# Two node stages of a graph attention kernel: merges by head with the residual in them, and eight PSUM banks in the last stage

## The chip, the cores and the metric

The kernel runs on one core of one Trainium2 chip. The metric is the device time of one execution in microseconds (us). The names of the engines in the rows are PE (TensorE), PEld (its weight loads), DVE (VectorE), ACT (ScalarE), POOL (GpSimd) and SP (SyncE, which issues the DMAs of the node stages); a q behind a name, as in DVEq or SPq, is that engine's sequencer.

## The reference

Three graph attention layers over 6,250 nodes with 256 features and 100,000 edges: two of a GATv2 block with 4 heads of 64 channels, then one of a GAT block with 8 heads of 32. Each block ends in a residual and a layer norm.

```python
def _gatv2_layer(x, src, dst, n, Wl, Wr, att, b):
    ...
    msg = xl[src] * alpha[:, :, None]
    out = jax.ops.segment_sum(msg, dst, num_segments=n)
    return out.reshape(n, H * C) + b
...
x = _layernorm(x + _L0_gnn_ref(x, edge_index, ...), axis=-1)
x = _layernorm(x + _L1_gnn_ref(x, L1_gnn_W, L1_gnn_a, src, dst), axis=-1)
```

In a GATv2 layer each node also has an edge to itself (a loop), and its message is what the kernel calls a node's own row.

## The kernel before

The nodes lie in 49 tiles of 128. The program goes through four node stages (`node_dve(l)`, `node_pe(l)` and so on, l = 0 to 3) with an edge stage between each two of them. An edge stage gathers rows by indirect DMA, scores them, and adds weighted rows into `acc`, 128 partitions by 49 tiles by 264 words. This change touches the node stages with l = 2 (the third stage) and l = 3 (the last).

A node stage is a software pipeline over tiles, written by `tiles(eng, (part, lag), ..., ring=R)`: at step t each engine runs its parts in the order of the list, each for tile t - lag. Buffers are taken in turn, tile t has buffer t % R. The first steps are written out, the middle ones are a hardware loop (`Fori`) whose body is R steps, the last are written out again. Every engine has a queue of its own and executes it strictly in order; engines meet by semaphores alone.

**Third stage (l = 2).** It ends layer two, makes the first layer norm, and the products of layer three. Per tile:
- SP loads the node's own row `own` (L490) and the residual row `res` of x (L492), and stores the projected table row (L504, lag 8) and the normalised row `hx_dram` (L508, lag 6): four DMAs a tile, each about 130 KB.
- DVE, for two tiles at once (`merged_two`): `own` = `own` times the loop's weight `wx` (L1342), `tmp` = `acc` times the weight `wn` (L1343), wait, `tmp` = `tmp` + `own` (L1345). Weights are spread over the 64 channels of a head by a zero step. Then `stats` (lag 2): bn_stats (L1372) and bn_aggr (L1374), one tile each. At the front of an even step stands `finish` (lag 4): a reciprocal of the root (L1384) and -mean/std (L1387), for two tiles.
- ACT: `normal` (lag 4, L758) writes the normalised tile from PSUM, `root` (lag 2, L767) takes the square root for two tiles, L790 and L792 copy products, L774 copies a transposed tile.
- PE: `products` (lag 5, L987), `turn_h` (lag 4, L974), then `residual`: a bias product (L957) and the product of `res` with the identity (L958), then `total`: `tmp` times the identity (L962), all summed in one of four PSUM banks.
- POOL clears `acc` of each merged tile (L630) and a part of x3 (L628), behind `acc_read`, which the merge raises.

**Last stage (l = 3).** SP loads `res` from `hx_dram` (L492) and stores the output (L501, lag 6). DVE runs `finish` (lag 4), `merged_two` (one tensor_tensor for two tiles, L1337) and `stats` (lag 2); ACT `normal` and `root`; PE `residual` (L958) and `total` (L962), in four banks. PE waits for `h_ready` of tile t - 4 before it opens a bank again, and DVE's `finish` waits for `std_ready`, which ACT's `root` raises when both `bn_aggr` of the pair have run.

## Time and profile before

| | before |
|---|---|
| median of 3 runs | 4010.43 us (4007.61 to 4011.79) |
| profiled execution, its own time | 4004.83 us |
| its span | 4003.0 us |
| PE, DVE, ACT, POOL busy | 88%, 82%, 32%, 69% of the span |
| third stage, first merge to last merge | 2647.6 to 2779.8 us |
| last stage, first merge to last merge | 3914.8 to 3993.7 us |

The span is what the profiler saw from the first to the last instruction; 1.8 us of the execution's own time lie outside it. Nearly all of the span is in the three edge stages, which the change does not touch. What it touches are about 147 us (the third stage, from its first merge to its last store) and 88 us (the last). A row of a timeline gives the start, the time taken, the engine, the line, the operation, what it writes and reads, and in brackets how long the engine had been idle and what ended that.

### The profile page before, as it was taken

The page shows a single profiled execution, that of the slowest core. Times are in us where ns is not written, and L with a number is a line of the kernel's source. Part 1 is how long each engine was busy: PE and PEld are TensorE (multiplying, and loading weights), DVE is VectorE, ACT ScalarE, POOL GpSimd, SP SyncE. Part 2 cuts the span into 40 slices and gives each one's busy share as a digit, 9 for nine tenths or more (in the row PEclk, how much of TensorE's full clock was granted, in tenths as well). Part 3 has the DMA queues.
Part 4 walks back from the last instruction along what each step waited for, and adds up shares of the span by engine and source line. Part 5 has one row for each costly group of instructions (what it writes and reads, how often), then busy time and mean ns, then how long its engine had stood idle before and what let it go on. Part 6 is the DMA issues. An engine that isn't in the chain of part 4 may idle for free. (4 is left out here: it accounts for less than half of the span.)

```text
span 4003.0 us, 115501 instructions
## 1 busy us (share of the span) xinstructions
PE 3522.5 (88%) x30761; PEld 2584.0 (65%) x30762; DVE 3296.9 (82%) x10046; ACT 1278.9 (32%) x4356; POOL 2765.2 (69%) x3039
## 2 busy tenths in 40 slices
PE   6699999999999668999999999977678888787885
PEld 5577777777777456777777777745445555555543
DVE  6768888888888885888888888876688898888886
ACT  4433333333333463333333333324111111111113
POOL 5577777777776467777777777723777777777760
PEclk9899999999999899999999999989799999899989
DMA  4344444444443124444444444435455555555544
GB/s 99 116 131 136 136 131 136 136 135 132 134 136 106 58 70 135 136 135 131 136 136 135 131 136 136 131 96 186 134 143 140 143 145 143 141 144 138 144 109 129
DMA packets 279405, 520.84 MB, mean 130 GB/s; under 512 B 98391, under 2 KB 165121, under 8 KB 279313
## 3 DMA queue, kind: packets, MB, share of 16 engines
q0 software_dynamic: 120320, 338.39, 31.2%
q1 hardware_dynamic: 158993, 181.36, 15.1%
q8 instruction: 41, 0.67, 0.1%
q14 instruction: 51, 0.42, 0.0%
HBM read 484.05 MB, written 35.46 MB: 130 GB/s over the span
## 5 line engine op out<-in xcount | busy, mean ns | idle before, releaser
L704 POOL DMA_INDIRECT gathered<-table,idx x2496 | 2501.4, 1002 | 787.6 <-issue 526.0
L1120 PE MATMUL pS<-gathered,Dm 128*128 128x264 f32 x4992 | 1689.5, 422 | 107.7 <-DVE Dm L1533 58.9
L1520 DVE TENSOR_TENSOR acc_mem<-acc_mem,pS 128x264 f32 x2496 | 1043.6, 418 | 144.8 <-PE pS L1120 105.6
L1059 PE MATMUL pZ<-DT,x 128*128 128x128 bf16 x9984 | 1090.2, 221 | 14.1 <-DVE DT L1480 11.5
L1059 PEld LDWEIGHTS pZ<-DT,x 128*128 x9984 | 874.2, 98 | 325.0 <-issue 51.7
L873 ACT ACTIVATE reluT<-pZ 128x256 f32<-128x256 f32 x1664 | 637.1, 383 | 1128.5 <-PE pZ L1065 1098.6
L1120 PEld LDWEIGHTS pS<-gathered,Dm 128*128 128x128 f32 x4992 | 797.2, 200 | 239.5 <-DVE gathered L1551 104.9
L1065 PE MATMUL pZ<-ident,gathered 128*128 128x128 f32 x3328 | 934.6, 281 | 11.9 <-DMA gathered<-table,idx 11.8
L1551 DVE TENSOR_TENSOR gathered<-gathered 128x256 f32<-128x256 f32 x2496 | 941.6, 417 | 1.8 <-ACT gathered L865 1.0
L1533 DVE TENSOR_TENSOR Dm<-pS,rel_items 128x256 f32<-128x256 f32 x1239 | 513.8, 415 | 0.0
L1065 PEld LDWEIGHTS pZ<-ident,gathered 128*128 128x128 f32 x3328 | 470.4, 141 | 16.2 <-DMA gathered<-table,idx 14.3
L1051 PEld LDWEIGHTS pL<-DT,x 128*128 x2496 | 236.0, 105 | 217.5 <-issue 116.5
L1051 PE MATMUL pL<-DT,x 128*128 128x128 bf16 x2496 | 324.7, 236 | 37.5 <-ACT first_row L859 28.5
L1073 PE MATMUL pL<-reluT,attpad 128*32 128x128 f32 x6656 | 269.2, 280 | 0.1
L1565 DVE TENSOR_TENSOR_SCAN F<-flags,cT 128x128 f32<-128x128 f32 x156 | 67.4, 432 | 216.6 <-ACT cT L858 214.8
L987 PE MATMUL pS<-W,gathered 128*128 128x260 f32 (+1 forms) x588 | 174.3, 421 | 36.1 <-ACT gathered L774 34.1
L1073 PEld LDWEIGHTS pL<-reluT,attpad 128*32 128x32 f32 x6656 | 156.9, 109 | 51.1 <-ACT reluT L873 0.9
L617 POOL TENSOR_TENSOR pool_pad<-zeros 128x1 f32<-128x1 f32 x184 | 54.6, 297 | 194.4 <-DVE gathered L1345 120.7
L841 ACT ACTIVATE lin<-gathered 128x128 f32<-128x128 f32 x52 | 21.8, 418 | 444.9 <-DMA gathered<-table,idx 444.9
L987 PEld LDWEIGHTS pS<-W,gathered 128*128 128x128 f32 x588 | 104.9, 198 | 75.9 <-ACT gathered L774 55.0
L1480 DVE TENSOR_SCALAR DT<-DT,iota_part 128x2048 bf16<-128x2048 bf16 x156 | 117.1, 750 | 12.4 <-DMA DT<-rel_dram 12.3
L1088 PE MATMUL pL<-ident,lin 128*128 128x128 f32 x156 | 53.1, 340 | 77.1 <-ACT lin L841 77.0
(230 smaller groups left out, 3211.4 us busy)
## 6 DMA issues: line engine op xcount, KB each, us to landing
DT<-rel_dram SPq DMA_DIRECT2D x156, 512.0 KB
gathered<-table,idx POOLq DMA_INDIRECT x2496
table<-xls SPq DMA_DIRECT2D x147, 132.0 KB, 2.0
flags<-flag_dram SPq DMA_DIRECT2D x416, 32.0 KB
flags<-flag_dram SPq DMA_DIRECT2D x52, 256.0 KB
gathered<-table SPq DMA_DIRECT2D x98, 132.0 KB, 2.1
gathered<-in_x SPq DMA_DIRECT2D x98, 128.0 KB, 2.1
hx_dram<-gathered SPq DMA_DIRECT2D x49, 128.0 KB, 1.7
```

Of the source, the lines that this page charges most:

```text
L704: nc.gpsimd.indirect_dma_start(out=G[:, b, i, :], out_offset=None, in_=tab[l], in_offset=bass.IndirectOffsetOnAxis(ap=idx[:, b, i:i + 1], ...
L873: nc.scalar.activation(relu_slot(i), z_slot(i), ACT.Relu).then_inc(relu_done, 1)
L987: mm = nc.tensor.matmul(pX[:, b, 0:width], hT[:, b, q * P:(q + 1) * P], W[:, q, 0:width], start=(q == 0), stop=(q == 1))
L1051: mm = nc.tensor.matmul(pL[:, 0:P], s3[:, bass.ds(tk[i], 1), s, GI - 1 - i:9 * GI - 1 - i].rearrange("p o c -> p (o c)"), moving, start=(i ...
L1059: mm = nc.tensor.matmul(z_slot(i)[:, half], x3[:, bass.ds(tk[i], 1), s, half].rearrange("p o c -> p (o c)"), moving, start=(s == 0), stop= ...
L1065: mm = nc.tensor.matmul(z_slot(i)[:, half], G[:, b, i, half], ident[:], is_transpose=True, start=False, stop=True)
L1073: nc.tensor.matmul(pL[a * (P // Q):(a + 1) * (P // Q), 0:P], attpad[:, q, ATT0 - k:ATT0 - k + P // Q], relu_slot(Q * k + a)[:, q * P:(q + ...
L1120: nc.tensor.matmul(pS[:, i % 4, 0:ROW], Dm[:, i % 8, :], G[:, at[0], at[1], :], start=True, stop=True).then_inc(seg_done, 1)
L1480: v.tensor_scalar(DT[:, b, :], DT[:, b, :], iota_part[:, 0:1], None, ALU.is_equal).then_inc(dt_ready, 1)
L1520: link(v.tensor_tensor(acc_at(n), acc_at(n), pS[:, n % 4, 0:ROW], ALU.add))
L1533: ins = v.tensor_tensor(Dm[:, 2 * p % 8:2 * p % 8 + 2, :], numbers.unsqueeze(1).to_broadcast([P, 2, P]), rel.unsqueeze(2).to_broadcast([P, ...
L1551: ins = v.tensor_tensor(gv, gv, row[:, D:D + H].unsqueeze(2).to_broadcast([P, H, D // H]), ALU.mult)
```

## The change

In the last stage the sums take eight PSUM banks in place of four, and `residual` loads go into eight buffers (`res8`). The ring is eight, so a bank is opened again behind tile t - 8. DVE's order at an even step becomes `merged_two`, `finish`, `stats`. Stores have lag 11; the normalised tiles still go through four buffers.

In the third stage the merge goes by tile and head: for each tile and each of 4 heads `own` = `own` times `wx` + `res`, one scalar_tensor_tensor over 128x64 whose weight is a pointer scalar in SBUF; behind a wait, `tmp` = `acc` times `wn` + `own` in the same form. `acc_read` is raised behind each tile. The residual product with the identity falls away, the bias product stays. SP's loads wait for `acc_read` of tile t - 4 in place of `sum_ready`.

The buffers are laid out anew in the same space. Cut to what matters:

```diff
-        pSum = [pS[:, 2, 0:D], pS[:, 3, 0:D], pL[:, 0:D], pM[:, 0:D]]
+        pSum = [pS[:, 2, 0:D], pS[:, 3, 0:D], pL[:, 0:D], pM[:, 0:D],
+                pS[:, 0, 0:D], pS[:, 1, 0:D], pZ[:, 0, 0:D], pZ[:, 1, 0:D]]
...
-                        else:
-                            sp.wait_ge(sum_ready, t + ((l - 2) * TILES - 3))
+                        elif l == 2:
+                            sp.wait_ge(acc_read, t + ((l - 1) * TILES - 3))
...
+                    if l == 3:
+                        if not (static(t) and t < 8):
+                            sp.wait_ge(sum_ready, t + (TILES - 7))
+                        sp.dma_start(res8[:, b, :], hx_dram[rows(t), :]).then_inc(res8_in[b], 16)
...
-                    tiles(sp, (load, 0), (store, 6), ring=4)
+                    tiles(sp, (load, 0), (store, 11), ring=8)
...
-                    tiles(act, (normal, 4), (root, 2), ring=4)
+                    tiles(act, (normal, 4), (root, 2), ring=8)
...
                 def residual(t, b, h):
-                    pe.wait_ge(res_in[b], (h + (l - 2) * QUARTER[b] + 1) * 16)
-                    if not (static(t) and t < 4):
-                        pe.wait_ge(h_ready, t + ((l - 1) * TILES - 3))
                     if l == 2:
+                        if not (static(t) and t < 4):
+                            pe.wait_ge(h_ready, t + (TILES - 3))
                         nc.tensor.matmul(pSum[b], ones_bf, bias3, start=True, stop=False)
-                    nc.tensor.matmul(pSum[b], ident[:], res[:, b, :], start=(l == 3), stop=False)
+                    else:
+                        pe.wait_ge(res8_in[b], (h + 1) * 16)
+                        if not (static(t) and t < 8):
+                            pe.wait_ge(h_ready, t + (2 * TILES - 7))
+                        nc.tensor.matmul(pSum[b], ident[:], res8[:, b, :], start=True, stop=False)
...
                         for k in range(n):
                             dve.wait_ge(own_in[b + k], (h + (HALF[b + k] if b + k < 2 else 0) + 1) * 16)
-                        mine = by_head(own[:, of, 0:D])
-                        v.tensor_tensor(mine, mine, spread_heads(wx), ALU.mult)
-                        v.tensor_tensor(by_head(tmp[:, of, :]), by_head(num), spread_heads(wn), ALU.mult).then_inc(node_step, n)
+                            dve.wait_ge(res_in[b + k], (h + 1) * 16)
+                            for j in range(H):
+                                of = slice(j * C, (j + 1) * C)
+                                ins = v.scalar_tensor_tensor(own[:, b + k, of], own[:, b + k, of], wx[:, bass.ds(t + k, 1), j],
+                                                             res[:, b + k, of], ALU.mult, ALU.add)
+                        ins.then_inc(node_step, n)
                         dve.wait_ge(node_step, t + ((l - 1) * TILES + n))
-                        v.tensor_tensor(tmp[:, of, :], tmp[:, of, :], own[:, of, 0:D], ALU.add).then_inc(acc_read, n)
+                        for k in range(n):
+                            num = acc[:, bass.ds(t + k, 1), 0:D].rearrange("p o r -> p (o r)")
+                            for j in range(H):
+                                of = slice(j * C, (j + 1) * C)
+                                ins = v.scalar_tensor_tensor(tmp[:, b + k, of], num[:, of], wn[:, bass.ds(t + k, 1), j],
+                                                             own[:, b + k, of], ALU.mult, ALU.add)
+                            ins.then_inc(acc_read, 1)
...
-                else:
+                elif l == 2:
                     tiles(dve, (finish, 4), (merged_two, 0), (stats, 2), ring=4)
+                else:
+                    tiles(dve, (merged_two, 0), (finish, 4), (stats, 2), ring=8)
```

How the queues change, at two places (a row is a line of the kernel, the operation, what it writes and reads and its shape, and what it waits for; `x3` stands for three equal ones). DVE in the third stage, the pair of tiles 4 and 5, ahead of the loop. Before:

```order
L1384 RECIPROCAL gathered<-gathered 128x2 [waits std_ready]
L1387 SCALAR_TENSOR_TENSOR gathered<-gathered 128x2 [waits rstd_step]
L1342 TENSOR_TENSOR gathered<-gathered 128x2x256 [waits own_in1,own_in0,sum_ready]
L1343 TENSOR_TENSOR gathered<-acc_mem,gathered 128x512
L1345 TENSOR_TENSOR gathered<-gathered 128x512 [waits node_step]
L1372 BN_STATS gathered<-pL 128x6 [waits sum_ready]
```

Of the change (its own line numbers; L1412 and L1415 are the two of `finish`, L1400 is bn_stats):

```order
L1412 RECIPROCAL gathered<-gathered 128x2 [waits std_ready]
L1415 SCALAR_TENSOR_TENSOR gathered<-gathered 128x2 [waits rstd_step]
L1363 SCALAR_TENSOR_TENSOR gathered<-gathered 128x64 [waits res_in0,own_in0,sum_ready]
L1363 SCALAR_TENSOR_TENSOR gathered<-gathered 128x64 x3
L1363 SCALAR_TENSOR_TENSOR gathered<-gathered 128x64 [waits res_in1,own_in1]
L1363 SCALAR_TENSOR_TENSOR gathered<-gathered 128x64 x3
L1371 SCALAR_TENSOR_TENSOR gathered<-acc_mem,gathered 128x64 [waits node_step]
L1371 SCALAR_TENSOR_TENSOR gathered<-acc_mem,gathered 128x64 x7
L1400 BN_STATS gathered<-pL 128x6 [waits sum_ready]
```

Three operations have become sixteen, and the merge now also waits for the residual's DMA. In the loop each of the sixteen has a register instruction for its address ahead of it.

DVE in the last stage, from the statistics of tiles 0 and 1 on. Before:

```order
L1372 BN_STATS gathered<-pS 128x6 [waits sum_ready]
L1374 BN_AGGR gathered<-gathered 128x2 [waits stat_step]
L1384 RECIPROCAL gathered<-gathered 128x2 [waits std_ready]
L1387 SCALAR_TENSOR_TENSOR gathered<-gathered 128x2 [waits rstd_step]
L1337 TENSOR_TENSOR gathered<-acc_mem,gathered 128x512 [waits sum_ready]
L1372 BN_STATS gathered<-pL 128x6 [waits sum_ready]
```

Of the change (L1355 is the merge):

```order
L1400 BN_STATS gathered<-pS 128x6 [waits sum_ready]
L1402 BN_AGGR gathered<-gathered 128x2 [waits stat_step]
L1355 TENSOR_TENSOR gathered<-acc_mem,gathered 128x512 [waits sum_ready]
L1412 RECIPROCAL gathered<-gathered 128x2 [waits std_ready]
L1415 SCALAR_TENSOR_TENSOR gathered<-gathered 128x2 [waits rstd_step]
L1400 BN_STATS gathered<-pL 128x6 [waits sum_ready]
```

The merge has moved between the statistics and the reciprocal that waits for ACT's root of them.

## Rows read from the trace of the kernel before

**Rows 1.** Stretches: length; busy us (count) of PE, PEld, DVE, ACT, POOL; clock, DMA.
```profile
2662.18:2682.89 20.71, 17.60 (x74) 13.26 (x75) 13.81 (x38) 9.17 (x31) 8.17 (x24) 0.83 0.56 168
2682.89:2779.80 96.91, 82.39 (x396) 61.26 (x395) 62.27 (x163) 47.10 (x163) 36.70 (x108) 1.00 0.64 195
3923.06:3993.68 70.62, 43.30 (x173) 30.06 (x173) 47.38 (x155) 28.87 (x66) 0.00 (x0) 1.00 0.52 158
```
**Rows 2.** Groups by line: merges in 2682.88 to 2779.78 and 3923.05 to 3993.67 us.
```profile
L1342 DVE TENSOR_TENSOR gathered<-gathered 128x512 f32<-128x512 f32 x18 | 12.5, 692 | 17.8 <-DMA gathered<-table 17.5 <-issue 0.3
...
L1337 DVE TENSOR_TENSOR gathered<-acc_mem,gathered 128x512 f32 (+1 forms) x22 | 15.2, 693 | 3.7 <-issue 3.7
```
**Rows 3.** Timeline of the third stage, DVE, one pair: start us, us, what.
```profile
2716.01 0.69 DVE L1342 TENSOR_TENSOR gathered<-gathered 128x512 f32<-128x512 f32 x1 [1.50 <-DMA gathered<-table]
...
2718.02 0.42 DVE L1372 BATCH_NORM_STATS2 gathered<-pL 128x6 f32<-128x256 f32 x1
...
2719.98 0.17 DVE L1384 RECIPROCAL gathered<-gathered 128x2 f32<-128x2 f32 x1 [0.56 <-DVEq L357]
2720.29 0.16 DVE L1387 SCALAR_TENSOR_TENSOR gathered<-gathered 128x2 f32<-128x2 f32 x1
2721.06 0.69 DVE L1342 TENSOR_TENSOR gathered<-gathered 128x512 f32<-128x512 f32 x1 [0.60 <-DMA gathered<-table]
```
**Rows 4.** Waits in 2640 to 2800 us, and PE's residual product in the timeline.
```profile
PEld pS L987 <- ACT gathered L774: 31.3, 35, 1.8
```
```profile
2718.16 0.60 PE L958 MATMUL pS<-gathered,ident 128*128 128x256 f32 x2
```
**Rows 5.** Prices: timeline and groups by line of VectorE operations elsewhere in the program.
```profile
4.25 4.03 DVE L1158 TENSOR_SCALAR x<-acc_mem 112x832 bf16<-112x832 f32 x7
...
3801.21 0.75 DVE L1551 TENSOR_TENSOR gathered<-gathered 128x256 f32<-128x256 f32 x2
...
L1551 DVE TENSOR_TENSOR gathered<-gathered 128x256 f32<-128x256 f32 x2496 | 941.6, 417 | 1.8 <-ACT gathered L865 1.0 <-ACT gathered L863 0.8
...
L1158 DVE TENSOR_SCALAR x<-acc_mem 112x832 bf16<-112x832 f32 x7 | 4.0, 647 | 0.0
...
L1250 DVE SCALAR_TENSOR_TENSOR DT<-DT,ident 128x256 bf16<-128x256 bf16 x1 | 0.5, 485 | 0.0
```
**Rows 6.** Timeline, DVE and POOL: a meeting early in the stage, and POOL later.
```profile
2650.03 1.06 POOL L628 CAST x<-zeros 128x429 bf16<-128x429 f32 x1
...
2650.61 1.03 DVE L1343 TENSOR_TENSOR gathered<-acc_mem,gathered 128x512 f32<-128x512 f32 x1
...
2718.32 0.54 POOL L628 CAST x<-zeros 128x429 f32 x1
```
**Rows 7.** Timeline of the last stage, DVE, one pair.
```profile
3961.33 0.16 DVE L1387 SCALAR_TENSOR_TENSOR gathered<-gathered 128x2 f32<-128x2 f32 x1
3961.68 0.69 DVE L1337 TENSOR_TENSOR gathered<-acc_mem,gathered 128x512 f32 x1 [0.19 <-issue]
3962.29 0.43 DVE L1372 BATCH_NORM_STATS2 gathered<-pL 128x6 f32<-128x256 f32 x1
...
3963.50 0.18 DVE L1374 BATCH_NORM_AGGREGATE gathered<-gathered 128x2 f32<-128x6 f32 x1
3964.24 0.17 DVE L1384 RECIPROCAL gathered<-gathered 128x2 f32<-128x2 f32 x1 [0.56 <-DVEq L357]
```
**Rows 8.** Timeline of the last stage, SP's issues.
```profile
3962.11 0.34 SPq L492 DMA_DIRECT2D gathered<-hx_dram  x1
...
3963.38 0.34 SPq L492 DMA_DIRECT2D gathered<-hx_dram  x1
```
**Rows 9.** Timeline at the start of the last stage, DVE.
```profile
3922.63 0.17 DVE L1384 RECIPROCAL gathered<-gathered 128x2 f32<-128x2 f32 x1 [1.84 <-DVEq L357]
...
3923.67 0.43 DVE L1372 BATCH_NORM_STATS2 gathered<-pL 128x6 f32<-128x256 f32 x1
...
3924.72 0.18 DVE L1374 BATCH_NORM_AGGREGATE gathered<-gathered 128x2 f32<-128x6 f32 x1
```

More of the change, by code:

```diff
@@ L153, in gnn_program @@
         zs = in_g(2, D)
-        zsum = in_g(2, 8)
+        res = in_g(4, D)
+        g_at[0] -= 4 * D
+        res8 = in_g(8, D)
+        g_at[0] -= 4 * D
         own = in_g(4, ROW)
-        res = in_g(4, D)
         tmp = in_g(4, D)
+        hbuf = in_g(4, D)
         ex = in_g(2, D)
         nd = in_g(6, 4 * TILES)
-        small = in_g(16, 8).rearrange("p (s b) k -> p s b k", s=4)
+        small = in_g(32, 8)
+        zsum = small[:, 0:2, :]
+        small = small.rearrange("p (s b) k -> p s b k", s=4)
         assert g_at[0] <= 2 * GI * ROW
@@ L222, in gnn_program @@
         res_in = [sem(f"res_in{b}") for b in range(4)]
+        res8_in = [sem(f"res8_in{b}") for b in range(8)]
         h_ready = sem("h_ready")
@@ L391, in by_two, with by_four @@
             return b % 2, h * 2 + b // 2
+        def by_four(b, h):
+            return b % 4, h * 2 + b // 4
         def static(v):
@@ L490, in load @@
                         sp.dma_start(own[:, b, :], tab[l - 1][rows(t), :]).then_inc(own_in[b], 16)
-                    if l in (2, 3):
-                        sp.dma_start(res[:, b, :], (x if l == 2 else hx_dram)[rows(t), :]).then_inc(res_in[b], 16)
+                    if l == 2:
+                        sp.dma_start(res[:, b, :], x[rows(t), :]).then_inc(res_in[b], 16)
+                    if l == 3:
+                        if not (static(t) and t < 8):
+                            sp.wait_ge(sum_ready, t + (TILES - 7))
+                        sp.dma_start(res8[:, b, :], hx_dram[rows(t), :]).then_inc(res8_in[b], 16)
                 def store(t, b, h):
@@ L498, in store @@
                         if static(t) and t == TILES - 1:
-                            sp.dma_start(out[t * P:N, :], hbuf[0:LAST, b, :]).then_inc(out_stored[b], 16)
+                            sp.dma_start(out[t * P:N, :], hbuf[0:LAST, b % 4, :]).then_inc(out_stored[b % 4], 16)
                         else:
-                            sp.dma_start(out[rows(t), :], hbuf[:, b, :]).then_inc(out_stored[b], 16)
+                            sp.dma_start(out[rows(t), :], hbuf[:, b % 4, :]).then_inc(out_stored[b % 4], 16)
                         return
@@ L756, in normal @@
                         else:
-                            act.wait_ge(out_stored[b], h * 16)
-                    nc.scalar.activation(hbuf[:, b, :], pSum[b], ACT.Identity, scale=small[:, 3, b, 0:1],
+                            b4, h4 = by_four(b, h)
+                            act.wait_ge(out_stored[b4], h4 * 16)
+                    nc.scalar.activation(hbuf[:, b % 4, :], pSum[b], ACT.Identity, scale=small[:, 3, b, 0:1],
                                          bias=small[:, 3, b, 1:2]).then_inc(h_ready, 1)
@@ L952, in residual @@
                 def residual(t, b, h):
[L953 to L955 removed]
                     if l == 2:
+                        if not (static(t) and t < 4):
+                            pe.wait_ge(h_ready, t + (TILES - 3))
                         nc.tensor.matmul(pSum[b], ones_bf, bias3, start=True, stop=False)
[L958 removed]
+                    else:
[3 more added lines that the diff above has]
+                        nc.tensor.matmul(pSum[b], ident[:], res8[:, b, :], start=True, stop=False)
                 def total(t, b, h):
                     pe.wait_ge(acc_read, t + ((l - 1) * TILES + 1))
[L962 removed]
+                    nc.tensor.matmul(pSum[b], ident[:], tmp[:, b % 4, :], start=False, stop=True).then_inc(sum_ready, 1)
                 def turn_h(t, b, h):
@@ L1011, in node_pe @@
                 else:
-                    tiles(pe, (residual, 0), (total, 0), ring=4)
+                    tiles(pe, (residual, 0), (total, 0), ring=8)
             def edge_pe(l):
@@ L1324, in merged_two @@
                     n = pair(t)
-                    of = slice(b, b + n)
+                    of = slice(b % 4, b % 4 + n)
                     def by_head(ap):
@@ L1369, in stats @@
                     dve.wait_ge(sum_ready, t + ((l - 2) * TILES + 1))
-                    if not (static(t) and t < 4):
-                        dve.wait_ge(h_ready, t + ((l - 1) * TILES - 3))
+                    if not (static(t) and t < (8 if l == 3 else 4)):
+                        dve.wait_ge(h_ready, t + ((l - 1) * TILES - (7 if l == 3 else 3)))
                     v.bn_stats(small[:, 0, b, 0:6], pSum[b]).then_inc(stat_step, 1)
@@ L1441, in node_dve @@
                     tiles(dve, (combine, 0), (elu, 1), (self_add, 5))
+                elif l == 2:
+                    tiles(dve, (finish, 4), (merged_two, 0), (stats, 2), ring=4)
                 else:
-                    tiles(dve, (finish, 4), (merged_two, 0), (stats, 2), ring=4)
+                    tiles(dve, (merged_two, 0), (finish, 4), (stats, 2), ring=8)
                 if l == 2:
```

3 lines of the change are left out of this document (1 added, 2 removed).

## Prediction

> **What bounds the kernel now.** Start with the busy time by stretch [rows 1]: the change touches two node stages only, so everything is argued from their stretches. From the merge of tiles 4 and 5 to that of tile 48 the third stage takes 20.7 + 96.9 us. PE is busy 82.4 of the 96.9, which looks like the bound. The last stage takes 70.6 us, with DVE busy 47.4 and PE 43.3, so there nobody is full, and a loop of waits sets the pace.
>
> The groups by line count the merges: 18 in the 96.9 us and 22 in the 70.6 us [rows 2], so a pair of tiles takes 5.38 us in the third stage and 3.21 us in the last. The same rows say what DVE waits for in the third stage: own rows' DMAs, 17.5 us, near 1 us a pair.
>
> The timeline of DVE in the third stage [rows 3] gives its chain, the loop that matters. Merge start to first bn_stats: 2.01 us. First bn_stats to the reciprocal: 1.96 us, with 0.56 us of idle at its end, when the reciprocal waits for ACT's root of the statistics just made. Reciprocal to L1387: 0.31 us. From there to the next merge 0.77 us here, 0.60 of it idle for a DMA; without that I put 0.45 us (0.35 us from L1387 to the merge in the last stage [rows 7], and two more semaphores). Together 2.01 + 1.96 + 0.31 + 0.45 = 4.73 us. So of 5.38 us a pair only some 0.65 us are slack on DVE. PE is no bound in spite of its 85%: its weight loads for L987 wait 31.3 us for ACT's copies [rows 4], and those stand behind the root in ACT's queue, and so behind DVE. SP's queue, with four DMAs a tile, is near its own limit too, but it issues the same DMAs afterwards.
>
> In the last stage the chain is the same [rows 7]: L1387 to the merge 0.35 us, merge to bn_stats 0.61, first bn_stats to the second bn_aggr 1.21, from there to the reciprocal 0.74, of which 0.56 us idle. With 0.32 us to L1387 that is 3.23 us.
>
> **Third stage: the residual product goes.** 49 products of two passes at 0.60 us [rows 4], 29 us of PE's work. I cost it at nothing: PE waits for ACT and DVE, and keeps waiting. Its cover is that idle time; were PE the bound, this would be the gain (a rival below).
>
> **Third stage: the merge by heads.** Three operations a pair leave (2.01 us up to bn_stats), sixteen of 128x64 with a pointer scalar come. The trace has no such operation, so I bound it. Two tensor_tensors of 128x256 take 0.75 us, one 417 ns [rows 5]: the second starts 0.333 us behind the first, and they overlap by 0.083 us. Two of 128x512 start 0.61 us apart, as the merge and the bn_stats behind it do [rows 7]. So an element costs 0.277/256 = 1.08 ns, and an operation 0.056 us besides. Lower end: 64 elements that way, 0.125 us apart. A scalar_tensor_tensor with a pointer scalar in SBUF takes 485 ns for 256 elements [rows 5], 68 ns more than the 417 of a tensor_tensor. Seven pointer operations in a row (L1158) take 4.03 us, one alone 647 ns: 0.564 us apart, an overlap of the same 0.083 us, so the 68 ns are not hidden by the next one. Upper end: no overlap at all, 0.28 us (485 - 192 x 1.08). I take 0.125 + 0.068, rounded to 0.20 us apart, and 0.28 us for the last of a row. The register instruction ahead of each fits beside it, since the operation ahead covers it, as those ahead of L1337 fit beside L1387 and cost 0.19 us for three [rows 7].
>
> Per pair: eight up to the wait, 7 x 0.20 + 0.28 = 1.68 us; semaphore and the next start 0.17 us; eight more up to bn_stats 8 x 0.20 + 0.05 = 1.65 us. Together 3.5 us for 2.01, so +1.5 us. The chain becomes 6.22 us.
>
> The residual's DMA is now waited for on DVE. It is issued some 0.55 us behind own's, but the second tile's rows are needed 0.8 us later than before, and DVE is now later anyway: nothing.
>
> **Third stage: POOL.** Early in the stage a merge operation took 1.03 us where its kind takes 0.69 us, while POOL's cast ran, itself 1.06 us in place of 0.54 [rows 6]: where two such operations meet, one waits for the other. Before, `acc_read` came at the end of the merge, and POOL's copies ran beside bn_stats, which reads PSUM (2718.32, beside the bn_stats from 2718.02 [rows 3, 6]). Now the first tile's `acc_read` comes 0.8 us before the merge ends, and the cast of 0.54 us falls into the last four operations. I put 0.45 us a pair on the chain, and keep 0 (copies just miss) and 0.7 us as ends. The Trainium skill, SBUF — State Buffer, section SBUF: two separate sides, says a VectorE operation with two SBUF inputs and a GpSimd operation that reads SBUF exclude each other for a whole instruction; the row agrees.
>
> So a pair costs 6.22 + 0.45 = 6.67 us. 18 pairs at 6.67 - 5.38 = +23.2 us. The four pairs ahead of them (20.7 us, 5.18 each) run without register work: at 6.4 us +4.9 us. The first two merges, ahead of the long reciprocal, +1.5 us each: +3. Third stage: **+31 us**. SP's earlier wait for `acc_read` gives nothing, for its queue no longer sets the pace.
>
> On the price of an operation the skill speaks another way. VectorE: DVE Perf Modes, section on the TRN2 errata, gives 58 cycles and one per element at 0.96 GHz, an estimate of 127 ns for 64 elements; by it the sum would be that of the rival "hidden" below. The pointer rows [rows 5] contradict it by 0.07 us an operation. The same page's rules say to minimise the number of operations, which speaks against this change.
>
> **Last stage: order and banks.** With the merge between the statistics and the reciprocal, the 0.74 us up to the reciprocal hold 0.61 us of work. Per pair: merge to reciprocal 0.61, reciprocal to L1387 0.31, to bn_stats 0.25 (two register instructions, an estimate from the 0.35 us with three), statistics 1.21, on to the merge 0.40: 2.78 us. The loop's branch was hidden in that wait and is now bare, an estimated 0.36 us for each four pairs: 2.87 us. For 16 pairs in the loop 16 x (3.23 - 2.87) = 5.8 us. Six pairs are now written out, where two statistics took 1.05 us [rows 9] and no registers are computed: 0.61 + 0.31 + 0.11 + 1.05 + 0.25 = 2.33 us, for 5.4 us more; at the start 0.6 us, because DVE sat idle 1.84 us there [rows 9] and the merge fits in. That is 11.8 us; I take **-11.5 us**. The eight banks are what allows it: PE need not wait for `normal`. Next late is SP: a load and a store take 1.27 us [rows 8], 2.54 us a pair and some more for its branch, under 2.87. The gain could be as low as 6 us if it or the four output buffers bind, and 13 at most.
>
> **Sum.** +31 - 11.5 = +19.5 us. The profiled execution took 4004.83 us, 1.8 over its span; it becomes 4024.3. The median of the runs lies 5.6 us above it, so I predict **4030 us**. A measurement of this kernel can tell some 0.2%, 8 us, from no change.
>
> **Rivals.**
> - *As forecast, both costs there*: 4030 us. Chance 0.50.
> - *POOL misses the merge*: 22 pairs x 0.45 = 10 us less, 4020 us. For it: the copies have a wait of their own ahead of them. Chance 0.27.
> - *Hidden*: operations 0.125 us apart. A merge of 7 x 0.125 + 0.21 + 0.17 + 8 x 0.125 + 0.05 = 2.3 us adds 0.3, less than the 0.65 us of slack; with a little for POOL +6 us, less 11.5: 4005 us. Against it: the two pointer rows. Chance 0.10.
> - *Register work in series*: every operation about 0.28 us apart. 5.0 us for the merge, a pair 7.7 us with less from POOL: +51, less 11.5: 4050 us. Chance 0.09.
> - *Faster, PE's relief decides*: PE's 85% is the bound, and DVE's chain at 0.125 us an operation stays at 5.0 us. Then a pair falls from 5.38 to about 5.2 us: 22 x 0.2 = 4 us, and 11.5: 3995 us. It decides below 0.145 us an operation. Against it: PE's waits for ACT [rows 4]. Chance 0.04.
>
> The range 4015 to 4045 us holds the first two and the near half of the fourth, and leaves out 0.2. Faster by over 0.2%: the last rival and a part of "hidden", 0.05. Within 0.2%: the rest of "hidden" and the low end of the second, 0.15. Slower: 0.80.
>
> **What would show it.** Right: in the third stage scalar_tensor_tensors of about 280 ns, a row of eight in about 1.7 us, a pair every 6.2 to 6.7 us, DVE busier and no longer waiting for own rows, PE near 60% busy, some of them stretched while POOL casts. In the last stage the reciprocal follows the merge without idle time, and merges are 2.9 us apart. Wrong: merges of the third stage under 5.5 us apart, or the last stage still at 3.2 us a pair with SP or ACT ahead of the wait.

## The result, and the profile after

| | before | after |
|---|---|---|
| median | 4009.8 us (4007.19 to 4011.79, 6 runs) | 4024.89 us (4022.61 to 4028.05, 6 runs) |
| profiled execution, its own time | 4004.83 us | 4022.61 us |
| its span | 4003.0 us | 4020.8 us |

The ratio is 1.0039, 95% interval 1.0028 to 1.0049: **15 us slower**. The forecast was 4030 us (4015 to 4045), slower. The profiled executions lie 17.8 us apart, in their spans as in their own times; the forecast for the one after was 4024.3 us.

First the stretches of the kernel after, those of [rows 1] and the head of each stage (columns as there; the starts are merge starts):

```profile
2647.81:2665.52 17.71, 4.93 (x11) 2.46 (x11) 14.28 (x49) 2.18 (x4) 4.49 (x12) 0.50 0.28 84
2665.52:2690.92 25.40, 19.06 (x60) 13.00 (x61) 20.72 (x89) 9.26 (x31) 8.52 (x24) 0.64 0.45 137
2690.92:2807.76 116.84, 79.52 (x324) 55.16 (x323) 94.56 (x396) 47.18 (x163) 37.44 (x108) 0.90 0.52 162
3950.41:4010.84 60.43, 44.96 (x183) 32.66 (x182) 47.14 (x155) 29.81 (x66) 0.00 (x0) 1.00 0.57 179
```

The 18 pairs of the third stage that took 96.91 us take 116.84, 6.49 us a pair in place of 5.38, and DVE is now busy 81% of them (64% before), PE 68% (85%). The 22 pairs of the last stage take 60.43 us in place of 70.62. From the first to the last merge the third stage grew by 27.8 us (132.2 to 160.0), the last shrank by 12.4 (78.9 to 66.5). The rest of the 17.8 us is 0.2 ahead of them, 1.6 between the stages and 0.6 behind the last merge.

DVE's timeline in the third stage, the rows that answer to [rows 3]:

```profile
2710.55 1.66 DVE L1363 SCALAR_TENSOR_TENSOR gathered<-gathered 128x64 f32<-128x64 f32 x8
...
2714.41 0.42 DVE L1400 BATCH_NORM_STATS2 gathered<-pS 128x6 f32<-128x256 f32 x1
...
2716.28 0.17 DVE L1412 RECIPROCAL gathered<-gathered 128x2 f32<-128x2 f32 x1 [0.56 <-DVEq L363]
2716.60 0.16 DVE L1415 SCALAR_TENSOR_TENSOR gathered<-gathered 128x2 f32<-128x2 f32 x1 [0.15 <-DVEq L363]
2717.06 1.72 DVE L1363 SCALAR_TENSOR_TENSOR gathered<-gathered 128x64 f32<-128x64 f32 x8 [0.29 <-issue]
2718.97 2.09 DVE L1371 SCALAR_TENSOR_TENSOR gathered<-acc_mem,gathered 128x64 f32<-128x64 f32 x8 [0.19 <-DVE gathered L1363]
2720.98 0.42 DVE L1400 BATCH_NORM_STATS2 gathered<-pL 128x6 f32<-128x256 f32 x1
...
2722.93 0.17 DVE L1412 RECIPROCAL gathered<-gathered 128x2 f32<-128x2 f32 x1 [0.56 <-DVEq L363]
2723.26 0.16 DVE L1415 SCALAR_TENSOR_TENSOR gathered<-gathered 128x2 f32<-128x2 f32 x1 [0.15 <-DVEq L363]
2723.53 0.48 DVE L1363 SCALAR_TENSOR_TENSOR gathered<-gathered 128x64 f32<-128x64 f32 x2
```

The merge is two rows of eight, 3.86 and 3.92 us up to bn_stats in place of 2.01. The statistics up to the reciprocal still take 1.87 and 1.95 us with their 0.56 us of waiting. The wait for own rows' DMA is gone. Now POOL beside the second row of eight, and then the view of the two lines' instructions (count; shortest, median and longest in ns; first and last start). FUSED_REGOPS are the register instructions ahead of them:

```profile
2719.93 0.19 POOL L631 TENSOR_TENSOR pool_pad<-zeros 128x1 f32<-128x1 f32 x1 [4.33 <-DVE gathered L1371]
2720.06 0.58 POOL L642 CAST x<-zeros 128x429 f32 x1
```
```profile
L1363 DVE SCALAR_TENSOR_TENSOR gathered<-gathered x196: 271/279/553, 2647.8 to 2808.4; 128x64 f32<-128x64 f32 x196
L1363 DVEq FUSED_REGOPS  x160: 57/57/94, 2677.7 to 2802.5; - x160
...
L1371 DVE SCALAR_TENSOR_TENSOR gathered<-acc_mem,gathered x196: 276/280/565, 2650.0 to 2809.3; 128x64 f32<-128x64 f32 x196
```

An operation takes 280 ns and up to 565. POOL's small operation that carries the wait (L631) starts at 2719.93, just behind the first tile's four, its cast starts at 2720.06, and the row of eight takes 2.09 us where the row ahead of it took 1.66 to 1.72.

A pair of the last stage answers to [rows 7], and the start of the stage to [rows 9] (DVE's timeline):

```profile
3949.14 0.43 DVE L1400 BATCH_NORM_STATS2 gathered<-pS 128x6 f32<-128x256 f32 x1
...
3950.41 0.69 DVE L1355 TENSOR_TENSOR gathered<-acc_mem,gathered 128x512 f32<-128x512 f32 x1
...
3952.63 0.42 DVE L1400 BATCH_NORM_STATS2 gathered<-pL 128x6 f32<-128x256 f32 x1
...
3971.55 0.69 DVE L1355 TENSOR_TENSOR gathered<-acc_mem,gathered 128x512 f32 x1 [0.19 <-issue]
3972.16 0.16 DVE L1412 RECIPROCAL gathered<-gathered 128x2 f32<-128x2 f32 x1
...
3974.24 0.69 DVE L1355 TENSOR_TENSOR gathered<-acc_mem,gathered 128x512 f32 x1 [0.17 <-issue]
...
3977.42 0.69 DVE L1355 TENSOR_TENSOR gathered<-acc_mem,gathered 128x512 f32 x1 [0.67 <-issue]
```

The reciprocal follows the merge with no idle time, the pair shown takes 2.69 us, and once in four pairs (3974.24 to 3977.42) it is 3.18 us, with 0.67 us of idle time ahead of the merge, where the loop's branch and registers stand.

### The profile page after: what moved, and what is told of

It is laid out like the page before. It is cut to its first block and busy times, and to the rows that moved or that the text cites. A ratio compares the mean times of both kernels' runs of the same rounds, so it can differ in the third digit from the quotient of the medians.

```text
span 4020.8 us, 115692 instructions
## 1 busy us (share of the span) xinstructions
PE 3517.0 (87%) x30663; PEld 2574.7 (64%) x30664; DVE 3339.4 (83%) x10363; ACT 1278.5 (32%) x4356; POOL 2761.9 (69%) x3039
## 3 DMA queue, kind: packets, MB, share of 16 engines
q1 hardware_dynamic: 158993, 181.36, 14.9%
## 5 line engine op out<-in xcount | busy, mean ns | idle before, releaser
L1077 PE MATMUL pZ<-DT,x 128*128 128x128 bf16 x9984 | 1090.6, 221 | 14.2 <-DVE DT L1510 11.5
L1005 PE MATMUL pS<-W,gathered 128*128 128x260 f32 (+1 forms) x588 | 184.1, 440 | 61.2 <-ACT gathered L789 58.9
L631 POOL TENSOR_TENSOR pool_pad<-zeros 128x1 f32<-128x1 f32 x184 | 54.6, 297 | 222.4 <-DVE gathered L1371 152.1
```

The source lines that it names most:

```text
L1005: mm = nc.tensor.matmul(pX[:, b, 0:width], hT[:, b, q * P:(q + 1) * P], W[:, q, 0:width], start=(q == 0), stop=(q == 1))
L1077: mm = nc.tensor.matmul(z_slot(i)[:, half], x3[:, bass.ds(tk[i], 1), s, half].rearrange("p o c -> p (o c)"), moving, start=(s == 0), stop= ...
```

## The experiments

In the table a stage runs from its first to its last bn_stats. "Pair" is the mean of the 16 (third stage) or 14 (last) pairs in the middle of the stage; stages and pairs are read from the one profiled execution of each kernel. The kernels ran on several chips, and each ratio is to the kernel before on the same chip. Four kernels marked * ran on a chip on which the edge stages took some 1170 us longer in every kernel, the kernel before included (5179.78 us); the node stages ran there as elsewhere, so of these only the stages are read.

| kernel | time, us | ratio to before | third stage | pair | last stage | pair |
|---|---|---|---|---|---|---|
| before | 4009.8 | | 125.9 | 5.41 | 76.9 | 3.23 |
| after | 4024.89 | 1.0039 (1.0028 to 1.0049) | 150.0 | 6.50 | 64.9 | 2.81 |
| third_old | 3996.12 | 0.9966 (0.9952 to 0.9979) | 126.5 | 5.39 | 64.9 | 2.81 |
| third_old_2 | 3998.76 | 0.9968 (0.9956 to 0.9981) | 127.4 | 5.43 | 64.9 | 2.81 |
| last_old | 4035.84 | 1.0062 (1.0049 to 1.0076) | 150.7 | 6.51 | 77.3 | 3.23 |
| pair_release | 4015.88 | 1.0014 (1.0005 to 1.0024) | 141.5 | 6.08 | 64.9 | 2.82 |
| wide | 4014.60 | 1.0016 (1.0006 to 1.0025) | 140.9 | 6.12 | 64.9 | 2.81 |
| wide_late | 4008.61 | 0.9996 (0.9987 to 1.0006) | 137.4 | 5.88 | 64.9 | 2.81 |
| wide_store9 | 4014.33 | 1.0013 (1.0003 to 1.0022) | 140.9 | 6.16 | 64.9 | 2.81 |
| no_product | 4009.12 | 0.9997 (0.9988 to 1.0007) | 125.0 | 5.40 | 77.2 | 3.23 |
| order_only * | 5177.93 | 0.9993 (0.9974 to 1.0012) | 126.2 | 5.41 | 69.9 | 2.94 |
| banks_only * | 5176.14 | 0.9994 (0.9980 to 1.0008) | 126.6 | 5.42 | 74.6 | 3.18 |
| both_orders * | 5190.28 | 1.0023 (1.0011 to 1.0036) | 148.9 | 6.62 | 64.9 | 2.82 |
| immediate * | 5181.46 | 1.0007 (0.9992 to 1.0022) | 133.4 | 5.73 | 64.9 | 2.81 |

**third_old and last_old: the halves apart.** `third_old` is the kernel after with its third stage put back; `last_old` is the kernel before with the new third stage.

```diff
# third_old, against after
+                        pe.wait_ge(res_in[b], (h + 1) * 16)
...
+                        nc.tensor.matmul(pSum[b], ident[:], res[:, b, :], start=False, stop=False)
...
-                            dve.wait_ge(res_in[b + k], (h + 1) * 16)
-                            for j in range(H):
-                                of = slice(j * C, (j + 1) * C)
-                                ins = v.scalar_tensor_tensor(own[:, b + k, of], own[:, b + k, of], wx[:, bass.ds(t + k, 1), j],
-                                                             res[:, b + k, of], ALU.mult, ALU.add)
...
+                        mine = by_head(own[:, of, 0:D])
+                        v.tensor_tensor(mine, mine, spread_heads(wx), ALU.mult)
+                        v.tensor_tensor(by_head(tmp[:, of, :]), by_head(num), spread_heads(wn), ALU.mult).then_inc(node_step, n)
...
+                        v.tensor_tensor(tmp[:, of, :], tmp[:, of, :], own[:, of, 0:D], ALU.add).then_inc(acc_read, n)
```

> The last stage of the change alone; the third stage is merged as before, with the residual product on PE. Theory (the third stage costs about 28 us, the last gives about 12 back, and they add): 3998 us beside 4010 before, merges of the last stage 2.8 us apart, merges of the third 5.4 us apart as before. Rival (the last stage is only faster because the third one ran before it in another way, or the two stretches trade time over the edge stage between them): within 3 us of 4010.

> The third stage of the change alone; the last stage has four banks and its old order. Theory: 4010 + 28 = 4038 us, a pair of the third stage 6.5 us, a pair of the last 3.23 us. Rival (part of the third stage's loss belongs to the new layout or to eight banks): under 4030 us.

Both came out as the theory had it. On one chip, beside the kernel before at 4008.56 us, they stand at -12.4 and +27.3 us, and each stage is as long as in the kernel that it comes from, to 0.8 us. So the halves add up. `third_old` is 0.3% faster than the kernel before and, by the two ratios, 0.7% faster than the one after.

> The kernel `third_old` once more, beside the others: only the last stage of the change (eight PSUM banks, merge ahead of the reciprocal), third stage as before. Theory: again 12 to 14 us under the kernel before, a ratio of 0.9965 to 0.997. Rival (its gain on the first chip was the chip's): a ratio of 0.999 or more.

On another chip it came out the same. This is the version to keep.

**pair_release: what meeting POOL costs.** Both tiles' `acc_read` is raised at the end of the merge.

```diff
-                            ins.then_inc(acc_read, 1)
+                        ins.then_inc(acc_read, n)
```

> The change with one edit: the merge of the third stage raises acc_read for both tiles behind the last operation, not behind each tile. If the two stretched operations of a merge (about 560 and 420 ns for 280) come from meeting POOL's copies, they fall to 280 ns, a pair goes from 6.50 to about 6.1 us and the time falls by 22 x 0.4 = 8 us, to 4016. If they are stretched for a reason of DVE's own (the end of a row, the address work), they stay and the time is that of the change, or longer since PE and POOL start later.

Confirmed. The same line and a piece of DVE's and POOL's timelines in this kernel:

```profile
L1371 DVE SCALAR_TENSOR_TENSOR gathered<-acc_mem,gathered x196: 271/280/308, 2647.7 to 2798.3; 128x64 f32<-128x64 f32 x196
```
```profile
2719.87 1.66 DVE L1371 SCALAR_TENSOR_TENSOR gathered<-acc_mem,gathered 128x64 f32<-128x64 f32 x8 [0.20 <-DVE gathered L1363]
2721.44 0.43 DVE L1400 BATCH_NORM_STATS2 gathered<-pS 128x6 f32<-128x256 f32 x1
```
```profile
2721.74 0.55 POOL L642 CAST x<-zeros 128x429 f32 x1
```

No operation of L1371 is longer than 308 ns now, the row of eight takes 1.66 us in place of 2.09, and the cast runs beside bn_stats, which is not stretched. So one line placed otherwise is worth 0.42 us a pair and 8.5 us of the stage. The Trainium skill, SBUF — State Buffer, section SBUF: two separate sides, gives the rule for it: one side holds the shared port for a whole instruction where DVE has two SBUF inputs and GpSimd reads SBUF. The rows agree: stretched with two inputs in SBUF, not stretched for bn_stats, which reads PSUM.

**immediate: what an operation costs by itself.** The pointer weights become the constant 0.5, so this kernel leaves the loop's and the sum's weights out of the third stage.

```diff
-                                ins = v.scalar_tensor_tensor(own[:, b + k, of], own[:, b + k, of], wx[:, bass.ds(t + k, 1), j],
+                                ins = v.scalar_tensor_tensor(own[:, b + k, of], own[:, b + k, of], 0.5,
...
-                                ins = v.scalar_tensor_tensor(tmp[:, b + k, of], num[:, of], wn[:, bass.ds(t + k, 1), j],
+                                ins = v.scalar_tensor_tensor(tmp[:, b + k, of], num[:, of], 0.5,
```

> The change with the constant 0.5 in place of both pointer weights in the third stage's merge, so the weights are left out of the computation and the register instructions for them too. It prices the pointer scalar. Theory (an operation of 64 elements costs 0.125 to 0.135 us, the pointer 0.068 more): operations of 210 to 220 ns, 0.13 us apart, a merge of 16 about 1.1 us shorter, a pair 5.4 to 5.5 us, 4003 us. Rival (a small operation costs 0.20 us whatever its scalar): still 0.20 us apart and 4025 us.

From the views of the two lines, and two rows of eight in DVE's timeline:

```profile
L1363 DVE SCALAR_TENSOR_TENSOR gathered<-gathered x196: 209/218/557, 3523.3 to 3665.3; 128x64 f32<-128x64 f32 x196
L1371 DVEq FUSED_REGOPS  x160: 57/57/82, 3550.9 to 3661.9; - x160
```
```profile
3591.91 1.51 DVE L1371 SCALAR_TENSOR_TENSOR gathered<-acc_mem,gathered 128x64 f32<-128x64 f32 x8 [0.16 <-DVE gathered L1363]
...
3601.94 1.17 DVE L1363 SCALAR_TENSOR_TENSOR gathered<-gathered 128x64 f32<-128x64 f32 x8
```

A row of eight takes 1.17 us at 218 ns an operation, so they are (1.17 - 0.22) / 7 = 0.136 us apart; with the pointer 1.66 at 280 ns, (1.66 - 0.28) / 7 = 0.197 us. The pointer scalar costs 0.06 us an operation, sixteen times a pair, as the prediction read it from [rows 5]. The edit also takes the register instructions away ahead of L1363, so two more rows are needed to say which of the two it was. L1371 keeps its 160 here, and its row at 3591.91 has the same spacing, (1.51 - 0.56) / 7 = 0.136 us, with a last operation of 0.56 us that meets POOL. And in the kernel after, the pairs ahead of the loop have the pointer but no register instructions (the first of those in the view of L1363 above starts at 2677.7), and a row of eight takes 1.66 us there too:

```profile
2665.52 1.66 DVE L1363 SCALAR_TENSOR_TENSOR gathered<-gathered 128x64 f32<-128x64 f32 x8
```

So it is the pointer, and the register instructions cost nothing beside it. In the second half of the stage every other pair ran at 5.2 us and the rest at 6.2 to 6.5, because these wait within the merge for the second tile's residual rows (10.8 us in 13 waits in the stage), so the mean of 5.73 misses the expected 5.4 to 5.5. The Trainium skill, VectorE: DVE Perf Modes, in its section on the TRN2 errata, has 58 cycles and one per element, an estimate of 127 ns for 64 elements. The 136 ns apart come near to it; the 197 ns of the pointer form do not.

**wide: the same sum in few operations.** Four tensor_tensors of 128x512 for two tiles, with the residual still added on DVE.

```diff
+                        v.tensor_tensor(mine, mine, spread_heads(wx), ALU.mult)
+                        v.tensor_tensor(by_head(tmp[:, of, :]), by_head(num), spread_heads(wn), ALU.mult).then_inc(node_step, n)
...
+                        v.tensor_tensor(own[:, of, 0:D], own[:, of, 0:D], res[:, of, :], ALU.add).then_inc(wide_step, n)
+                        dve.wait_ge(wide_step, t + n)
+                        v.tensor_tensor(tmp[:, of, :], tmp[:, of, :], own[:, of, 0:D], ALU.add).then_inc(acc_read, n)
```

> The change with the merge of the third stage in four wide tensor_tensors per pair (own times its weight, sums times theirs, plus res, plus own), still with no residual product on PE. It tells the count of operations from the place of the residual. Theory (the price is sixteen small operations): one more operation of 0.61 us and one more wait of about 0.15 us than before, DVE's chain 4.73 + 0.75 = 5.5 us a pair, so the third stage is 2 to 4 us longer than before and the whole 4001 us. Rival (waiting for the residual's DMA on DVE is what costs): a pair stays over 6 us and the time over 4012.

Missed: 4014.6, not 4001 us. DVE's timeline:

```profile
2735.87 0.69 DVE L1362 TENSOR_TENSOR gathered<-gathered 128x512 f32<-128x512 f32 x1 [1.70 <-DMA gathered<-in_x]
...
2741.30 0.69 DVE L1362 TENSOR_TENSOR gathered<-gathered 128x512 f32<-128x512 f32 x1 [0.20 <-issue]
...
2748.54 0.69 DVE L1362 TENSOR_TENSOR gathered<-gathered 128x512 f32<-128x512 f32 x1 [2.06 <-DMA gathered<-in_x]
```

One pair takes 5.43 us, near the chain of 5.5 us that was computed; the next takes 7.24, because it stands 2.06 us for the residual's rows. SP's issues and ACT's timeline show why these are late: a store at 2741.09, 2.5 us behind the issue ahead of it, and the loads for two tiles only then.

```profile
2738.59 0.35 SPq L503 DMA_DIRECT2D gathered<-in_x  x1
2741.09 0.35 SPq L519 DMA_DIRECT2D table<-xls  x1
...
2745.65 0.35 SPq L501 DMA_DIRECT2D gathered<-table  x1
2746.19 0.35 SPq L503 DMA_DIRECT2D gathered<-in_x  x1
...
2748.08 0.35 SPq L501 DMA_DIRECT2D gathered<-table  x1
```
```profile
2740.18 0.30 ACT L783 ACTIVATE gathered<-gathered,eps_col 128x2 f32<-128x2 f32 x1 [3.33 <-ACTq L364]
...
2740.54 0.39 ACT L808 ACTIVATE xls<-pS 128x264 f32<-128x264 f32 x1
```

The store waited for ACT's copy (L808), ACT had stood 3.33 us ahead of its root (L783), and the root waits for DVE's statistics. SP also has little room of its own: one tile's four issues take 2.43 us where no wait holds them (2745.65 to 2748.08), an estimated 4.9 us a pair beside DVE's 5.43, so that a slip of 2 us is not soon made up. Two runs took this apart.

> The kernel `wide` with the wait for the residual's rows moved from the head of the merge to ahead of the third of its four operations, some 1.1 us later; same operations, same loads, same order of SP's queue. Theory (in `wide` every other pair stood at its head for the residual's DMA, 1.7 to 2.1 us on its rows, and only the two others ran at the chain's own pace of 5.43 us): the slow pairs lose 1.0 to 1.2 us each, the mean of all pairs goes from 6.12 to 5.5 to 5.6 us, the stage from 141 to 128 to 130 us, the whole from 4014.6 to 4002 to 4005 us. Rival (SP's queue and not the place of the wait sets these pairs: a store waits for ACT, the loads behind it are late by as much whatever DVE waits for): the wait only moves to own's rows or to the third operation, the mean stays at 6.0 us or more and the whole within 3 us of `wide`.

> The kernel `wide` with SP's store of `xls` in the third stage one tile later in its queue (lag 9 in place of 8), so that its wait for ACT no longer stands ahead of the next two loads; nothing else is moved. Theory (in `wide` the slow pairs are a loop through SP: the store waits for ACT's copy, the loads behind it come late, DVE waits for them, ACT waits for DVE): SP's waits for ACT's copy, 15.9 us in 2690 to 2795, fall under 3 us, DVE's waits for the residual's DMA under 4 us, a pair goes from 6.12 to 5.5 to 5.7 us, the stage from 141 to 128 to 132 us, the whole to 4002 to 4006 us. Rival (eight DMA issues a pair at about 0.6 us, some 5 us, fill SP's queue, so that any slip of it shows, whoever it waits for): the wait turns up at the hx store or as own rows' DMA, and a pair stays at 5.9 us or more.

```diff
# wide_late: the wait moves from ahead of own * wx to ahead of own + res
-                            dve.wait_ge(res_in[b + k], (h + 1) * 16)
...
+                        for k in range(n):
+                            dve.wait_ge(res_in[b + k], (h + 1) * 16)
# wide_store9
-                    tiles(sp, (load, 0), (store, 8), (keep, 6), ring=4)
+                    tiles(sp, (load, 0), (store, 9), (keep, 6), ring=4)
```

`wide_late` falls between its theory and its rival: a pair 5.88 us in the mean, with pairs of 5.33 and of 6.5. The total came down to that of the kernel before. The waits of DVE in 2690 to 2795 us (line waited for: us, times, longest) show that the wait went over to own's rows, as the rival had it, though smaller:

```profile
DVE gathered L1361 <- DMA gathered<-table: 8.6, 9, 1.2
```

`wide_store9` gained nothing (6.16 us a pair for 6.12), as its rival had it. DVE's wait for the residual stayed, and SP's moved from the store of `xls` to that of the normalised tile. SP's queue in `wide`, and below it in `wide_store9`, both in 2690 to 2780 us:

```profile
SPq L519 <- ACT xls L808: 13.7, 13, 2.0
```
```profile
SPq L523 <- ACT gathered L774: 15.0, 19, 1.9
```

So the theory "this store's place sets it" fell. Both of SP's stores wait for ACT, whose work stands behind the root, and whichever comes first holds up the loads. That the ring DVE, ACT, SP, DMA, DVE closes this way is read from the waits and not shown by a run without it. How much of it is the wait for ACT and how much the time of SP's eight issues a pair stays open.

**both_orders: can the third stage have the new order too?** `third_old` with `merged_two` ahead of `finish` in the third stage, on four banks.

```diff
-                    tiles(dve, (finish, 4), (merged_two, 0), (stats, 2), ring=4)
+                    tiles(dve, (merged_two, 0), (finish, 4), (stats, 2), ring=4)
```

> The last stage of the change, and the third stage merged as before but with the reciprocals behind the merge there too (four banks, ring of four). Theory (DVE's chain has 0.56 us of idle time there as well, but SP's queue and own rows' DMAs stand close behind at 5.1 to 5.4 us a pair): pairs of the third stage at 5.1 to 5.4 us, 3992 to 3998 us, at or a little under third_old. Rival (PE needs the banks earlier than normal frees them, now that it stands behind the merge): the third stage gets longer, 4000 us or more.

The time is the rival's: 6.62 us a pair, 22 us lost. Its cause, PE short of banks, does not show in the rows. DVE's row of the waits in 3560 to 3660 us, then SP's and PE's:

```profile
DVE gathered L1362 <- DMA gathered<-table: 39.7, 16, 2.6
```
```profile
SPq L522 <- ACT gathered L773: 23.2, 15, 1.8
```
```profile
PE pZ L994 <- ACT gathered L773: 21.5, 14, 1.7
```

`normal` now comes behind the merge, SP's store of the normalised tile waits for it, the next loads stand behind that store, and the next merge waits for them. It is the same ring with the merge in it. PE waits for `normal` too, but at `turn_h` (L994), which needs the normalised tile itself, so it is argued, and not run, that more banks alone would not free it. In the last stage the new order does not do this. A tile has two DMAs there and not four. The stores' lag of eleven is not what it takes, for `order_only` below has a lag of six and no wait of DVE for a DMA in its last stage.

**order_only and banks_only: the last stage's two parts.** `order_only` is the kernel before with the new order in the last stage and four banks; `banks_only` is `third_old` with the old order on eight banks. "Banks" stands for all that goes with them: the eight residual buffers, the ring of eight and the stores' lag of eleven, which no run parts.

```diff
# order_only, against before
+                elif l == 2:
+                    tiles(dve, (finish, 4), (merged_two, 0), (stats, 2), ring=4)
                 else:
-                    tiles(dve, (finish, 4), (merged_two, 0), (stats, 2), ring=4)
+                    tiles(dve, (merged_two, 0), (finish, 4), (stats, 2), ring=4)
```

> The kernel before with one edit: in the last stage DVE merges before it takes the reciprocals; four banks, ring of four. Theory (the banks are what allows the new order): PE opens a bank behind normal of tile t - 4, which now comes behind the merge of tile t, so sums come later and bn_stats of the next pair waits for PE; part of the gain only, pairs at 3.0 to 3.2 us, 4005 to 4009 us. Rival (the order is the whole gain): pairs at 2.8 us, 3998 us.

> Third stage as before; last stage with eight banks and eight residual buffers, but with the reciprocals ahead of the merge as before. Theory (the wait for the root sets the pace, not the banks): pairs at 3.23 us, 4010 us, within 2 us of the kernel before. Rival (PE's wait for an open bank sets the pace): pairs under 3.0 us, 4000 us or less.

The stage goes from 76.9 us to 69.9 by the order alone, to 74.6 by the banks alone, to 64.9 by both: -7.0, -2.3, and 2.7 us more when they are together. `order_only` lies between its theory (3.0 to 3.2 us a pair) and its rival (2.8) at 2.94; `banks_only`, 3.18 us a pair, is near its theory, and 1.4 of its 2.3 us fall in four pairs at the stage's start (2.82 to 2.89 us), where the ring of eight has more steps written out. In `order_only` pairs of 2.76 and 3.13 us alternate. The timelines say what the slow ones wait for (DVE first, then ACT and PE ahead of it):

```profile
5138.10 0.69 DVE L1337 TENSOR_TENSOR gathered<-acc_mem,gathered 128x512 f32 x1 [0.52 <-PE pL L962]
```
```profile
5136.11 0.56 ACT L758 ACTIVATE gathered<-pL,gathered 128x256 f32<-128x256 f32 x1 [0.49 <-DVE gathered L1387]
5136.73 0.30 PEld L958 LDWEIGHTS pL<-gathered,ident 128*128 128x128 f32 x2 [0.33 <-ACT gathered L758]
...
5137.27 0.59 PE L962 MATMUL pL<-gathered,ident 128*128 128x256 f32 x2
```

With four banks PE waits for ACT's `normal` to free one, `normal` waits for DVE's -mean/std, and DVE's merge for PE's sum. With the eight banks that wait of the merge is gone. The prediction had said that they are what allows the gain; they add 5.0 of the 12.0 us, the order gives 7.0 without them.

**no_product: PE's relief alone.** The kernel before without the residual product of the third stage; its output leaves that residual out.

```diff
-                    nc.tensor.matmul(pSum[b], ident[:], res[:, b, :], start=(l == 3), stop=False)
+                    if l == 3:
+                        nc.tensor.matmul(pSum[b], ident[:], res[:, b, :], start=(l == 3), stop=False)
```

> The kernel before with one thing taken out: PE's product of identity and residual in the third stage. The output leaves out that stage's residual; every DMA stays, and so do all waits of DVE, ACT and SP. Theory of the prediction (PE waits for ACT and DVE in this stage, the product is hidden): a pair of tiles in the third stage stays at 5.4 us, the stage from the first to the last bn_stats at 125 to 126 us, the whole at the time of before within 2 us. Rival (PE is the bound at its 85%, and 0.6 us a tile come back): a pair at 5.2 us or less, the stage at 122 us or less, the whole 4 us or more faster.

The third stage of this kernel by stretch, from the first to the last bn_stats, and below it the same of the kernel before:

```profile
2659.85:2784.81 124.96, 89.69 (x401) 60.57 (x401) 80.19 (x213) 60.74 (x204) 45.94 (x135) 0.96 0.60 184
```
```profile
2658.64:2784.51 125.87, 104.59 (x492) 78.31 (x493) 80.21 (x213) 60.95 (x204) 45.94 (x135) 0.96 0.59 182
```

PE's busy share falls from 83% to 72%, and a pair goes from 5.41 to 5.40 us. The ratio, 0.9997, holds no gain that can be measured, and the 0.9 us of the stage are no more than it varies without an edit to it (125.9 to 127.4 us in `before`, `third_old`, `third_old_2`, `order_only` and `banks_only`).

## Why the prediction was right

The sign, the mechanism and the size came out: 4024.89 for 4030 us. Of the 5.1 us between them 1.7 lie in the profiled execution (4022.61 for 4024.3). The other 3.4 are the step from it to the median, put at 5.6 us by the kernel before and 2.3 us here. That the first part is so small is in part luck: the third stage was put 3.2 us too high and the last stage's gain 0.9 us too low, and against these 4.1 us stand 2.4 us outside both stages, which no step had. Step by step:

- **The operation's price: right.** 0.197 us apart and 0.28 us for the last were forecast as 0.20 and 0.28. That the pointer's cost shows fully was the choice on which all hung, and `immediate` shows it: at the 0.136 us without it, sixteen operations are 1 us shorter. The rival "hidden" needed that price, and "register work in series" fell too: 160 register instructions of 57 ns stand ahead of L1363's operations, and a row of eight takes 1.66 us with them and without. (That rival's merge adds up to 4.7 us and not 5.0, so by its own terms it stood at 4044 us, not 4050.)
- **POOL: right in kind, near in size.** 0.45 us a pair was put down, `pair_release` measures 0.42. The rival "POOL misses the merge" is refuted by the same run: that is what its kernel does, and by the two ratios it is 0.2% faster than the one after.
- **The pair: 6.49, not 6.67 us.** The term that was mis-sized most is the step from L1387 (now L1415) to the next merge. I had taken 0.45 us for it, with "two more semaphores"; it is 0.46 us in one pair (2716.60 to 2717.06) and 0.27 in the next (2723.26 to 2723.53), 0.09 us less in the mean. The merge (3.86 and 3.92 us for 3.95) and the statistics (1.87 and 1.95 for 1.96) are 0.05 us less each. Over 18 pairs it makes 19.9 us where 23.2 were forecast.
- **The four pairs ahead and the first two merges: right.** 25.40 - 20.71 = +4.7 us for +4.9, and 17.71 - 14.55 = +3.2 for +3. Third stage together +27.8 for +31.
- **The residual product at nothing: right**, by `no_product`. Its size on PE was not: 49 x 0.60 = 29 us was counted, and PE's busy time fell by 14.9 us. A part is overlap: in the kernel before the next product starts 0.43 us behind this one (2718.16 to 2718.59), which makes 21 us; the rest was not traced. It had no effect here, but in a stage bound by PE the forecast would have had nearly twice the time that PE was relieved of.
- **The last stage: -12.4 for -11.5 us.** By bn_stats it is -12.0. The start gave 0.64 us (3949.14 to 3952.63 in place of 3919.54 to 3923.67) for 0.6. Five written-out pairs run at 2.24 to 2.54 us and not six at 2.33, 4.3 us where 5.4 were forecast, and the last two pairs gave 0.4 us that was in no step. The pairs in the loop take 2.81 us in the mean where 2.87 were forecast, with the branch measured at 3.18 - 2.69 = 0.49 us every four pairs and not 0.36, and a pair without it at 2.69 to 2.79, not 2.78.
- **"SP's queue no longer sets the pace": right for this kernel, and only for it.** DVE's merges in the third stage wait 0.5 us for the residual's DMA in all, and not for own rows. But every shorter merge that was tried ran into SP: `immediate`, `wide`, `wide_late` and `wide_store9` each have pairs 1 us or more over their chain. My expectation for `wide` took DVE's chain as the whole story, though the waits for own rows in [rows 3] had shown that other loop one step behind.
- **PE near 60% busy: wrong.** It is 68% (79.52 of 116.84 us), at a granted clock of 0.90 in place of 1.00.
- The 0.2 us ahead of the third stage, 1.6 between the stages and 0.6 at the end were in no step, and what caused them stays open.

## What to carry to other kernels

Before folding several wide VectorE operations into many small ones with a pointer scalar, multiply the count by the spacing of such operations, and here that was 16 x 0.2 us against three operations of 0.69 us, of which two in a row start 0.61 us apart. The engine that is relieved gains nothing as long as it waits: find the row that names what it waits for. Where a semaphore is raised in the middle of a row of operations, look at what it sets off on the engine that shares a port; and when a chain has been shortened, look for the queue that was one step behind, since a later wait only moves there.

## What was not expected of the hardware

- The granted clock of PE fell in the third stage, from 1.00 [rows 1] to 0.90, between its two levels of 2.4 and 1.2 GHz, where PE had become less busy (68% for 85%). By 20 us stretches of the kernel after it is 0.83 in one and 1.00 in the next:

```profile
2710.00:2730.00 20.00, 14.67 (x55) 10.41 (x56) 15.98 (x68) 8.60 (x30) 6.24 (x18) 0.83 0.51 160
2730.00:2750.00 20.00, 11.92 (x56) 8.19 (x57) 16.24 (x69) 8.21 (x28) 6.24 (x18) 1.00 0.52 160
```

  Pairs run at 6.41 and 6.6 us in turn through both, so it costs nothing as long as DVE sets the pace. In `no_product`, with PE at 72% of the stage, it was 1.00 from 2682.89 to 2779.80.
- A program can run 1170 us longer on another chip, and all of it in one kind of stage. There POOL's indirect loads in the edge stages stood idle 2001.6 us where they did 787.6 us in the kernel before on the first chip, as this row of the groups of `immediate` has it; why was not looked into:

```profile
L718 POOL DMA_INDIRECT gathered<-table,idx x2496 | 2443.5, 979 | 2001.6 <-POOLq L363 1422.3
```
